# Last stage of a decoder kernel: how three queues fetch the two expert results of every batch

## The reference

```python
gate_logits = x.mean(axis=1) @ gate_w.T + gate_b
_, top_idx = jax.lax.top_k(gate_logits, K)                     # K = 2 of E = 4
gate_weights = jax.nn.softmax(gate_logits, axis=-1)
mask = jnp.zeros_like(gate_weights).at[jnp.arange(x.shape[0])[:, None], top_idx].set(1.0)
expert_outs = jax.vmap(_encoder_layer, ...)(x, ...)
ffn = jnp.einsum('be,ebsd->bsd', gate_weights * mask, expert_outs)
x = _layernorm(x + ffn, axis=-1)
```

## Time and profile before

| | us |
|---|---|
| median of 3 runs | 7091.52 |
| lowest and highest | 7090.75, 7101.0 |
| the profiled execution | 7091.58 |
| its span in the profile | 7089.8 |
| in it, the last stage from its first DMA issue to the end | 166.9 |

### The profile page before, as it was taken

One profiled execution on the slowest core, in us unless ns is written; L12 is line 12 of the kernel. 1 busy time (PEld: TensorE's weight loads), 2 busy tenths in 40 slices (PEclk: granted clock), 3 DMA queues, 4 the chain that ended last, 5 costly groups with the idle time before them and its releaser, 6 DMA issues. The chain is left out here.

```text
span 7089.8 us, 153477 instructions
## 1 busy us (share of the span) xinstructions
PE 5269.5 (74%) x51100; PEld 3020.4 (43%) x51100; DVE 5405.9 (76%) x10078; ACT 3475.3 (49%) x4879; POOL 2891.1 (41%) x2616
## 2 busy tenths in 40 slices
PE   4777777777777765887778888799985656777790
PEld 1222222222222223565545555467664545666440
DVE  3999999999999984897845555477768975888444
ACT  3555556555555543565622222244445644777550
POOL 5333333434333313665600000155543335988543
PEclk8998888888888877998989999899997877999995
DMA  1111111111111112211110000000001111222343
GB/s 40 40 43 41 42 40 42 40 42 38 44 41 42 41 42 79 55 46 41 36 36 13 13 13 14 24 19 17 16 12 38 31 44 50 73 73 73 107 143 99
DMA packets 567447, 316.48 MB, mean 45 GB/s; under 512 B 60697, under 2 KB 557532, under 8 KB 566556
## 3 DMA queue, kind: packets, MB, share of 16 engines
q1 hardware_dynamic: 556700, 304.49, 15.5%
q10 hardware_dynamic: 7680, 3.15, 0.2%
q0 software_dynamic: 2560, 2.63, 0.1%
HBM read 169.59 MB, written 52.43 MB: 31 GB/s over the span
## 5 line engine op out<-in xcount | busy, mean ns | idle before, releaser
L1363 ACT ACTIVATE mb_dA<-ps,mb_a_neg 128x1024 f32<-128x1024 f32 x1008 | 1123.4, 1115 | 772.9 <-PE ps L1133 675.9
L1707 DVE TENSOR_TENSOR mb_m<-mb_dA,ps 128x512 f32<-128x512 f32 x2016 | 1284.1, 676 | 29.2 <-PE ps L1148 17.4
L1715 DVE TENSOR_TENSOR ps<-mb_m,ps 128x512 f32<-128x512 f32 x1984 | 1272.1, 684 | 41.8 <-PE ps L1148 41.5
L1148 PE MATMUL ps<-mb_ur,mb_bl 64*128 64x256 bf16 x4032 | 446.3, 305 | 525.1 <-DVE mb_m L1707 517.9
L1160 PE MATMUL ps<-mb_m,mb_cz 128*32 128x256 f32 x8064 | 732.9, 440 | 4.1 <-DVE mb_m L1707 3.1
L1148 PEld LDWEIGHTS ps<-mb_ur,mb_bl 64*128 64x128 bf16 x4032 | 121.6, 97 | 1063.1 <-DVE mb_m L1707 1000.1
L1133 PE MATMUL ps<-mb_ur,mb_sel 64*128 64x256 bf16 x4032 | 449.3, 306 | 122.1 <-ACT mb_dA L1363 97.2
L2400 DVE TENSOR_TENSOR mo_gu<-mo_gate,ps 128x512 f32<-128x512 f32 x288 | 195.6, 684 | 368.6 <-ACT mo_gate L2320 368.6
L2320 ACT ACTIVATE mo_gate<-ps 128x512 f32<-128x512 f32 x288 | 170.3, 597 | 537.3 <-PE ps L2261 537.2
L2260 PE MATMUL ps<-mo_hT,mo_wg 128*128 128x512 f32 x576 | 318.8, 637 | 128.3 <-DVE mo_gu L2400 128.3
L1133 PEld LDWEIGHTS ps<-mb_ur,mb_sel 64*128 64x128 bf16 x4032 | 154.0, 102 | 411.7 <-ACT mb_dA L1363 263.6
(11 more groups left out here) (452 smaller groups left out, 12889.4 us busy)
## 6 DMA issues: line engine op xcount, KB each, us to landing
mb_ur<-mb_pc SPq DMA_DIRECT2D x768, 64.0 KB
mb_bl<-mb_pc SPq DMA_DIRECT2D x576, 64.0 KB
ef_w<-in_ef_w SPq DMA_DIRECT2D x35, 514.5 KB
ea_wqk<-in_ea_wqk SPq DMA_DIRECT2D x70, 129.0 KB
ea_wvo<-in_ea_wvo SPq DMA_DIRECT2D x70, 128.5 KB, 2.2
ea_x<-hidden SPq DMA_DIRECT2D x280, 32.0 KB, 2.0
ea_ln_rows<-in_ea_ln SPq DMA_DIRECT2D x70, 128.0 KB, 3.0
pairs<-ea_y SPq DMA_DIRECT2D x70, 128.0 KB, 2.6
```

The source lines that it names most:

```text
L1148: mm = nc.tensor.matmul(ps[:, UB + 2 * (t % 2) + g, 256 * pl:256 * pl + 256], bl[k, j % 2, tl, 128 * pl:128 * pl + 128], ur[k, j % 2, tl], ...
L1363: nc.scalar.activation(dA[:, t % RING].rearrange("p (g n) -> p g n", g=2), ps[:, DT:DT + 2, :], ACT.Exp, scale=a_neg[:, 0:1]).then_inc(dA_ ...
L1707: nc.vector.tensor_tensor(m[:, t % RING, half], dA[:, t % RING, half], ps[:, UB + 2 * ((t - 1) % 2) + g, :], ALU.mult).then_inc(m_ready.se ...
L1715: nc.vector.tensor_tensor(u, m[:, t % RING, 512 * g:512 * g + 512], u, ALU.add).then_inc(h_ready.sem, 1)
```

## The change

The 16 fetches of 32 KB per chunk become 12. First results: SyncE gathers those of batches 0 to 3 and ScalarE those of batches 4 to 7, in blocks as before. Second results: POOL fetches them with four indirect DMAs per chunk, each of 128 rows of 512 bytes, one row for each partition. An indirect DMA takes its row numbers from SBUF, so the stage first computes a table `rows`: 64 times the slot plus the position (`place`, 0 to 63 twice). The slots for it come in two more loads, `second`, in the form of the gate loads; with the load of `place` they stand ahead of the gate loads on SyncE's queue. Three small DVE operations, at the start of the stage, turn them into `rows`. POOL waits for `rows` rather than for `slots`. Its loop is written out. One counter goes and two signals come.

```diff
--- before.py
+++ after.py
@@ -3398,12 +3398,16 @@
                 loop(dve, chunk)
 
 
-def combine(nc, sems, ps, x_in, t_in, x_out, plan):
+def combine(nc, sems, ps, place_in, x_in, t_in, x_out, plan):
 
     CHUNKS = TILES // 4
     with ExitStack() as mem:
         st = Stage(nc, sems, mem, "cb")
         slots = st.sb("slots", [1, 2 * B], I32)
+        second = st.sb("second", [128, TILES, 2], I32)
+        first_row = st.sb("first_row", [128, TILES])
+        rows = st.sb("rows", [128, TILES], I32)
+        place = st.sb("place", [128, 1])
         gate = st.sb("gate", [128, TILES, 2])
         x = st.sb("x", [128, 2, 4, 128])
         part = [st.sb(f"part{r}", [128, 2, 4, 128]) for r in range(2)]
@@ -3416,9 +3420,11 @@
         eps = st.sb("eps", [128, 4])
         seen = st.sb("seen", [128, 1])
         t_loaded = st.dma_signal("t_loaded")
-        passed = {q: st.counter(f"passed_{q}") for q in ("sp", "act", "pool")}
+        s_loaded = st.dma_signal("s_loaded", 3)
+        rows_ready = st.counter("rows_ready", 3)
+        passed = {q: st.counter(f"passed_{q}") for q in ("sp", "act")}
         g_loaded = st.dma_signal("g_loaded", 2)
-        loaded = [st.slot_signal("loaded0_", 6), st.slot_signal("loaded1_", 6)]
+        loaded = [st.slot_signal("loaded0_", 5), st.slot_signal("loaded1_", 4)]
         pool_loaded = [nc.alloc_semaphore(name=f"cb_pool_loaded{u}") for u in range(2)]
         st.handles.extend(pool_loaded)
         y_stored = st.slot_signal("y_stored")
@@ -3428,16 +3434,17 @@
         mv_ready = st.counter("mv_ready")
         rstd_ready = st.counter("rstd_ready", 2)
         y_ready = st.counter("y_ready")
+        rows_of = t_in.rearrange("n s d -> (n s) d")
         st.begin()
 
-        def gather(eng, queue, i, u, r, batches, landed):
+        def gather(eng, queue, i, u, batches, landed):
 
             eng.wait_ge(added.sem, added.at(i - 2))
 
             eng.sem_inc(passed[queue].sem, 1)
             for b in batches:
-                s = eng.value_load(slots[0:1, bass.ds(16 * i + (2 * b + r), 1)], min_val=0, max_val=SLOTS - 1)
-                eng.dma_start(part[r][64 * (b % 2):64 * (b % 2) + 64, u, b // 2],
+                s = eng.value_load(slots[0:1, bass.ds(16 * i + 2 * b, 1)], min_val=0, max_val=SLOTS - 1)
+                eng.dma_start(part[0][64 * (b % 2):64 * (b % 2) + 64, u, b // 2],
                               t_in[bass.ds(s, 1)].rearrange("a p d -> p (a d)")).then_inc(landed, 16)
 
         with nc.Block() as block:
@@ -3445,13 +3452,17 @@
             @block.sync
             def _(sp):
                 sp.dma_start(slots[:], plan["slot"].rearrange("(a b) r -> a (b r)", a=1)).then_inc(t_loaded.sem, 16)
+                sp.dma_start(place[:], place_in).then_inc(s_loaded.sem, 16)
+                for b2 in range(2):
+                    src = plan["slot"].rearrange("(t b) r -> b t r", b=2)[b2:b2 + 1]
+                    sp.dma_start(second[64 * b2:64 * b2 + 64], src.to_broadcast([64, TILES, 2])).then_inc(s_loaded.sem, 16)
                 for b2 in range(2):
                     src = plan["gate"].rearrange("(t b) r -> b t r", b=2)[b2:b2 + 1]
                     sp.dma_start(gate[64 * b2:64 * b2 + 64], src.to_broadcast([64, TILES, 2])).then_inc(g_loaded.sem, 16)
 
                 def load(i, u):
 
-                    gather(sp, "sp", i, u, 0, range(5), loaded[0].of(u))
+                    gather(sp, "sp", i, u, range(4), loaded[0].of(u))
                     sp.dma_start(x[:, u], tiles_of(x_in, i, 4)).then_inc(loaded[0].of(u), 16)
 
                 def store(i, u):
@@ -3474,21 +3485,26 @@
             def _(act):
                 act.wait_ge(t_loaded.sem, t_loaded.at(0))
                 for u in range(2):
-                    gather(act, "act", u, u, 1, range(6), loaded[1].of(u))
+                    gather(act, "act", u, u, range(4, 8), loaded[1].of(u))
                 with looped(nc, act, 1, CHUNKS // 2) as r:
                     for u in range(2):
-                        gather(act, "act", 2 * r + u, u, 1, range(6), loaded[1].of(u))
+                        gather(act, "act", 2 * r + u, u, range(4, 8), loaded[1].of(u))
 
             @block.gpsimd
             def _(pool):
                 nc.gpsimd.memset(half_neg[:], -0.5).then_inc(half_set.sem, 1)
                 nc.gpsimd.memset(eps[:], LN_EPS).then_inc(half_set.sem, 1)
                 pool.wait_ge(half_set.sem, half_set.at(0))
-                pool.wait_ge(t_loaded.sem, t_loaded.at(0))
+                pool.wait_ge(rows_ready.sem, rows_ready.at(0))
 
                 def fetch(i, u):
-                    gather(pool, "pool", i, u, 0, range(5, 8), pool_loaded[u])
-                    gather(pool, "pool", i, u, 1, range(6, 8), pool_loaded[u])
+                    if i >= 2:
+                        pool.wait_ge(added.sem, added.at(i - 2))
+                    for t in range(4):
+                        nc.gpsimd.indirect_dma_start(
+                            part[1][:, u, t], None, rows_of,
+                            bass.IndirectOffsetOnAxis(ap=rows[:, 4 * i + t:4 * i + t + 1], axis=0)).then_inc(
+                                pool_loaded[u], 16)
 
                 def scale(i):
                     pool.wait_ge(mv_ready.sem, mv_ready.at(i))
@@ -3498,21 +3514,26 @@
 
                 for u in range(2):
                     fetch(u, u)
-                with looped(nc, pool, 0, CHUNKS // 2 - 1) as r:
-                    for u in range(2):
-                        scale(2 * r + u)
-                        fetch(2 * r + (u + 2), u)
-                for u in range(2):
-                    scale(CHUNKS - 2 + u)
+                for i in range(CHUNKS):
+                    scale(i)
+                    if i + 2 < CHUNKS:
+                        fetch(i + 2, i % 2)
 
             @block.vector
             def _(dve):
+                dve.wait_ge(s_loaded.sem, s_loaded.at(0))
+                nc.vector.tensor_copy(first_row[:], second[:, :, 1]).then_inc(rows_ready.sem, 1)
+                dve.wait_ge(rows_ready.sem, rows_ready.at(0, 1))
+                nc.vector.tensor_scalar(first_row[:], first_row[:], 64.0, place[:, 0:1], ALU.mult, ALU.add).then_inc(
+                    rows_ready.sem, 1)
+                dve.wait_ge(rows_ready.sem, rows_ready.at(0, 2))
+                nc.vector.tensor_copy(rows[:], first_row[:]).then_inc(rows_ready.sem, 1)
                 dve.wait_ge(g_loaded.sem, g_loaded.at(0))
 
                 def chunk(i, u, g):
                     for r in range(2):
                         dve.wait_ge(loaded[r].of(u), loaded[r].at(i, u))
-                    dve.wait_ge(pool_loaded[u], 16 * 5 * (i // 2 + 1))
+                    dve.wait_ge(pool_loaded[u], 16 * 4 * (i // 2 + 1))
 
                     dve.wait_ge(y_ready.sem, y_ready.at(i - 1))
                     for t in range(4):
@@ -3601,6 +3622,7 @@
     a["rt_average"] = np.where(part[:, None] // 64 == np.arange(2)[None, :], f(1 / 64), f(0))
     a["rt_before"] = (part[:, None] < part[None, :]).astype(f)
     a["rt_number"] = np.repeat(part[:, None], 128, 1).astype(f)
+    a["cb_place"] = (part % 64).astype(f).reshape(128, 1)
     a["rt_iota"] = np.arange(SLOTS).astype(f)
     a["rt_chunk"] = (np.arange(SLOTS // 4) // 2).astype(f)
     a["ex_wg"], a["ex_bg"] = inp[t + "gate_w"].T, inp[t + "gate_b"]
@@ -3690,7 +3712,7 @@
             attention8(nc, sems, ps, "ea", src.rearrange("t (a s) d -> (t a) s d", a=2), tiles[0], w, qkv_bias=True,
                        tail="affine", plan=plan)
             expert_ffn(nc, sems, ps, dram, tiles[0], tiles[1], plan)
-            combine(nc, sems, ps, src, pairs[1], dst, plan)
+            combine(nc, sems, ps, dram["cb_place"], src, pairs[1], dst, plan)
 
         mamba(nc, sems, ps, dram, x, h[0])
         mlp(nc, sems, ps, dram, x, h[0], h[1])
```

## The result

| kernel | median us | lowest to highest | ratio to before, 95% interval |
|---|---|---|---|
| before | 7093.86 (22 runs) | 7085.45 to 7104.41 | |
| after | 7106.2 (22 runs) | 7093.32 to 7114.03 | 1.0015 [1.0008, 1.0021] |

The change makes the kernel slower by 0.15%, some 11 us of 7094 (the medians are 12.3 us apart). That is small, inside the 0.2% that the prediction called no change, but the interval excludes zero, and the sum had said -0.8 us. The profiled execution took 7110.64 us, with a span of 7108.7. In it the last stage begins with its first DMA issue at 6928.19 us, 4.9 us later than the first gate issue of before and 5.2 us later than the first issue of its stage (6922.95). The diff does nothing there, so 5.2 us of the 18.9 us between the two profiles are not its own. Inside the stage 180.5 us stand against 166.8, +13.7 us.

A forecast was written before the change was run, and what follows sets the result against it. The prediction took SyncE's DMA issuing in the last stage as the bound, 8.46 us per chunk. Terms +19.9, +0.4 and -21.1 us summed to -0.8 us, so 7090.8 us; stated range 7086 to 7130.

The forecast's parts named there:

- the sum: Whole kernel: start +19.9 and +0.4 us, SyncE's removed gathers -21.1 us, together -0.8 us.
- Step (e): Stage start: two loads of `second` cost +19.9 us, the small load +0.4 us, all ahead of the first chunk.
- Step (a): SyncE's queue: one gather fewer in each of 16 chunks, -21.1 us; interval from 8.46 to 7.13 us.
- Step (b): ScalarE's queue: two of six gathers fewer, 5.3 us per chunk; it was no bound, so worth 0.
- Step (c): DVE: chunk unchanged at 6.25 us, below the new pace; three small operations at the start are off the path.
- Step (d): POOL: four indirect fetches at 1.3 us (bounds 0.52 to 2.3) make 6.5 us, hidden under SyncE's 7.13 us.
- rival 1: POOL becomes the pace, each indirect fetch over 1.45 us; 7121 us at 2.0 us each; chance 0.28.
- POOL the pace: Same as rival 1: indirect fetches over 1.45 us set the interval; 7138 us at 2.3 us each; chance 0.28.
- POOL and DVE exclusive: DVE's two-input operations and POOL's indirect fetches block each other over SBUF; interval 10.3 us, 7135 us; chance 0.10.
- Cheap start: Loads of `second` run beside the gate loads and cost a few us; 7075 us; chance 0.04.
- the forecast case: Whole kernel: main case without rivals, 7090.8 us by the sum, 7088 to 7099 with its bounds; chance 0.58.

The follow-up runs named there:

- e4: after with `second` loaded as one DMA of 1 KB per partition instead of two loads of tiny pieces; 7072.95 us, ratio to before 0.9971.
- f2: e4 again on another chip (after with `second` as one 1 KB per partition load); 7088.29 us, ratio to before 0.9993.
- f3: e2 again on another chip (after with four plain POOL fetches from fixed rows); 7088.55 us, ratio to before 0.999.
- f1: after unchanged, run again on the same chip as f2, f3 and f4; 7107.4 us, ratio to before 1.0017.
- e2: after with POOL's four indirect fetches per chunk replaced by plain ones of the same size from fixed rows; 7086.68 us, ratio to before 0.9992.
- e3: after with two indirect fetches per chunk instead of four, two tiles used twice; 7088.24 us, ratio to before 0.9989.
- f4: e3 again on another chip (after with two indirect fetches per chunk); 7091.2 us, ratio to before 0.9998.
- e1: before with four instead of five gathers per chunk on SyncE, nothing else moved; 7090.53 us, ratio to before 0.9996.
- g4: before with `gate` alone loaded as one DMA of 1 KB per partition; 7080.05 us, ratio to before 0.9973.
- e9: after with seven more already-met waits ahead of SyncE's first gather, shifting its stream; 7102.67 us, ratio to before 1.0014.
- g2: after with the streams of SyncE and ScalarE exchanged, ScalarE also loading x and storing y; 7095.04 us, ratio to before 1.0.
- g3: after with `second` and `gate` as whole loads, SyncE three gathers, ScalarE five, POOL's fetches two and two; 7064.9 us, ratio to before 0.9949.

## Why the prediction failed, step by step

**Step (e), the start: right.** Forecast +19.9 and +0.4, less 1.3 for a gather fewer ahead of the first chunk, so 19.0 us later within the stage; measured 45.8 - 28.4 = 17.4, and taking the cause away took 17.6 back (e4, f2). Some 1.5 us of it go with the indirect fetches, since with plain ones the first chunk is at 44.3 and not at 45.8 (f3, f1). The rate of tiny pieces carried over to loads that weren't in the trace.

**Step (a), SyncE's gather: right in itself, and the sum's failed term.** Where nothing disturbs SyncE, the interval is 7.01 to 7.04 us (e2, e3, f3, f4) against 7.13 forecast. In after it is 8.24, and 8.08 and 8.09 when it ran again. The difference, some 1.1 us x 15 = 16 us (14 to 17 by the kernel), is what the sum lacked: of the 21.1 us that it took off SyncE, 2.4 came in the first profile. The step that failed is the assumption that the time of SyncE's issues, read beside POOL's direct gathers, is the same beside POOL's indirect ones. I had priced (d) on POOL alone, as an instruction that is hidden under SyncE's interval; its cost lay on the other engine, which set the pace. The prediction had a rival in which POOL's fetches disturb DVE, and none in which they disturb a queue.

**Step (b), ScalarE: right that it costs nothing, wrong in why it matters.** e1 shows that with six gathers ScalarE is the next bound, at about 8.1 us. "It was no bound" held for 8.46 us and not for 7.13.

**Step (c), DVE: right.** The two-input operations last 346 ns median, like 347 in the earlier trace rows. The tile part in after (duration ns, minimum/median/maximum):

```profile
L3504 POOL DMA_INDIRECT cb_part<-pairs,cb_rows x64: 940/955/1232, 6952.8 to 7090.3; - x64
...
L3540 DVE SCALAR_TENSOR_TENSOR cb_acc<-cb_part,cb_gate,cb_x x64: 338/346/376, 6974.0 to 7098.4; 128x128 f32<-128x128 f32 x64
L3545 DVE SCALAR_TENSOR_TENSOR cb_acc<-cb_part,cb_gate,cb_acc x64: 334/346/407, 6975.2 to 7099.5; 128x128 f32<-128x128 f32 x64
```

**Step (d), POOL: the price right, the packets wrong.** 0.955 us busy and steps of mostly 1.25 to 1.26 us, 1.38 behind a chunk's first fetch, where the prediction took 1.3 (bounds 0.52 to 2.3). Of its steps (start, us, idle before it):

```profile
7036.65 1.08 POOL L3504 DMA_INDIRECT cb_part<-pairs,cb_rows  x1 [0.19 <-issue]
7038.03 0.95 POOL L3504 DMA_INDIRECT cb_part<-pairs,cb_rows  x1 [0.30 <-issue]
7039.28 0.95 POOL L3504 DMA_INDIRECT cb_part<-pairs,cb_rows  x1 [0.30 <-issue]
```

The queue's 2048 packets over 64 fetches are 32 each, not 144: 16 of 4 KB and 16 that count. One packet for each row was a guess, and the high bound built on it (2.3 us) was what gave rival 1 its 0.28.

**The rivals.** POOL the pace: refuted, the fetch is under 1.45 us and POOL waits for DVE 15 times. POOL and DVE exclusive: refuted as a block. Of the 128 two-input operations 94 run beside a fetch of 955 ns; their median is 346 ns, like that of the others, and the longest is 407 ns. The rule of the Trainium skill (SBUF — State Buffer, Who interferes with whom), by which the later of the two blocks fully, isn't borne out for indirect DMAs here; the most that the trace shows is some lengthening of y's scaling beside a fetch (median 342 ns, longest 494). Cheap start: refuted by the 17.4 us.

**Size against sign.** e2 and f3 have after's start and bytes and no standstills. Their stages are 5.9 and 6.2 us shorter than before's, and their medians 6.4 and 5.9 us under before on their chips, where the sum had -0.8. Its own terms were off by little: +15.8 and +15.9 us at the start against 19.0, -20.4 and -20.9 in 15 intervals against 15 x 1.32 = 19.8, and -1.3 behind the last start, which it didn't have. On the same chip as f3 after's stage is 17.7 us longer: 16.3 in the intervals, 1.5 at the start; its median is 18.9 us higher. So the missing term is over three times the rest of the error, and of opposite sign. That 7106.2 us lies inside the stated 7086 to 7130 is luck: the forecast case ended at 7099, and what lies above was kept for a slow POOL, which didn't come.

**What is shown and what is not.** Shown, on one chip: with four indirect fetches for a chunk SyncE's issues stand still, with four plain ones or two indirect ones they don't (0 and 0.6 us). Excluded: the packets moved, the place in the stream, POOL's written-out loop, the late start. Not shown: what inside the chip holds the stream. The standstills begin mostly 0 to 2 us after the third or fourth fetch of a chunk, while its transfers run, and the DMA engines are far from full (0.37 in the window above). Why e4 had none stays open.

## What to carry to other kernels

When an engine is replaced as the fetcher, price the new instruction on the engine that sets the pace too, and not only on the one that issues it: here the hidden POOL fetches cost the neighbouring queue 1.1 us a chunk, nearly as much as the removed gather was worth. Before taking work off the pacing queue, work out the next queue's full cycle; ScalarE's was 0.3 to 0.4 us behind (e1). And read the start of a short stage first: one load in whole 1 KB rows in place of 8-byte pieces was worth more (17 us, g4) than what the change took off the steady part of after (2.4 us).

## What was not expected of the hardware

- An indirect DMA of 128 rows of 512 bytes costs POOL 0.955 us and a step of 1.25 us, against 0.534 us for a plain one of the same size (e2), and makes as many packets as the plain one, 32.
- With four of them for a chunk other queues' instruction streams stand still for 0.7 us at a time, 14 to 27 us over 15 chunks on SyncE (e9, g2), and up to 9.9 us on ScalarE (g3, two and two). On one of the five chips a kernel with them ran free of it.
- A load in pieces of 8 bytes holds its whole queue: from the first of two of 4,096 pieces to the end of the next issue it is 19.9 us, where the same values as one load of 1 KB per partition are issued in 0.35 us. The Trainium skill (DMA: Bandwidth & Descriptors, Issuing engines are not separate DMA queues) calls the sequencer's time to start a DMA usually small beside the DMA itself; in this stage it was the pace: 1.32 us for each gather from a register address on SyncE, while the DMA engines were at 0.38.
